# Attention on one Trainium2 core: a turn's score units, projections and small steps in another order

## What is computed

```python
q = (x @ Wq.T + bq).reshape(B, S, H, 2 * hd).transpose(0, 2, 1, 3)   # B 32, S 256, H 16, hd 8
k = (x @ Wk.T + bk).reshape(B, S, H, 2 * hd).transpose(0, 2, 1, 3)
v = (x @ Wv.T + bv).reshape(B, S, H, hd).transpose(0, 2, 1, 3)
q1, q2, k1, k2 = ...                          # two streams, each turned by _apply_rope
s1 = where(causal, neg, q1 k1^T * scale); s2 = where(causal, neg, q2 k2^T * scale)
attn = softmax(s1) - lam * softmax(s2)
out = attn @ v
out = out * rsqrt(mean(out * out) + EPS) * head_norm_w * (1 - LAMBDA_INIT)
x = x + out @ Wo.T + bo                       # x here is layer-normalised before q, k, v
```

## Time and profile before

| | |
|---|---|
| median of 3 runs | 1861.6 us (1861.06 to 1861.72) |
| device time of the profiled execution | 1863.29 us |
| its span, first to last instruction | 1861.6 us |
| mean granted TensorE clock | 0.968 of full speed |
| attention, from the first XT to the last store | about 450 to 1424 us of the span |
| one full turn of attention | 28.53 us |
| busy in the span | PE 86%, DVE 73%, ACT 68%, POOL 56% |

### The profile page before, as it was taken

The page is one execution under the profiler, slowest core; times in us unless marked ns, Lnnn a source line. Parts: engine busy times, 40 slices in busy tenths (PEclk is TensorE's granted clock), DMA queues, the critical chain, the costliest instruction groups (busy, mean ns, idle before and its releaser), DMA issues. The chain is left out here.

```text
span 1861.6 us, 43161 instructions
## 1 busy us (share of the span) xinstructions
PE 1608.8 (86%) x16448; PEld 1220.1 (66%) x16448; DVE 1363.2 (73%) x3442; ACT 1269.4 (68%) x1613; POOL 1046.3 (56%) x707
## 2 busy tenths in 40 slices
PE   4999999994588888888888888888873799999998
PEld 3787777883466666666666666666652577778787
DVE  5777777765778778878887788788742677777775
ACT  4777777772167767767677677677664577777776
POOL 4888888875324434334344343343312688888885
PEclk9999999997699999999999999999996799999999
DMA  3333323321323233232232332322302232233331
GB/s 113 103 114 115 102 88 108 109 103 46 87 79 92 58 91 82 66 94 72 76 94 61 86 87 60 95 78 70 89 12 77 97 115 90 93 114 110 108 109 63
DMA packets 142846, 163.14 MB, mean 88 GB/s; under 512 B 13244, under 2 KB 124558, under 8 KB 141454
## 3 DMA queue, kind: packets, MB, share of 16 engines
q1 hardware_dynamic: 142640, 160.38, 28.8%
HBM read 91.20 MB, written 14.70 MB: 57 GB/s over the span
## 5 line engine op out<-in xcount | busy, mean ns | idle before, releaser
L292 POOL TENSOR_TENSOR ffn_h_low<-ffn_h,ffn_h_high 128x1024 fp32r<-128x1024 f32 x192 | 458.4, 2401 | 95.0 <-ACT ffn_h_high L341 94.8
L1019 ACT ACTIVATE att_prob<-att_ring 128x1024 f32<-128x1024 f32 x384 | 388.6, 1022 | 155.9 <-PE att_ring L1240 153.4
L1125 DVE TENSOR_REDUCE att_nmax<-att_ring 128x4 f32<-128x1024 f32 (+1 forms) x384 | 450.8, 1217 | 54.3 <-PE att_ring L1240 54.3
L479 DVE TENSOR_TENSOR ffn_h<-ffn_up,ffn_comb_wide 128x1024 f32<-128x1024 f32 x256 | 311.3, 1216 | 125.1 <-ACT ffn_up L334 122.8
L334 ACT ACTIVATE ffn_up<-ffn_up 128x1024 f32<-128x1024 f32 x256 | 258.1, 1008 | 202.8 <-PE ffn_up L567 201.1
L341 ACT ACTIVATE ffn_h_high<-ffn_h 128x1024 fp32r<-128x1024 f32 x256 | 269.3, 1052 | 0.7 <-DVE ffn_h L479 0.7
L935 POOL TENSOR_TENSOR att_qk<-att_turned 128x512 f32<-128x512 f32 x64 | 81.4, 1273 | 318.0 <-DVE att_turned L1104 318.0
L1240 PE MATMUL att_ring<-att_qs,att_kd 64*128 64x256 bf16 (+1 forms) x2048 | 151.1, 249 | 95.4 <-DVE att_nmax L1125 57.2
L567 PE MATMUL ffn_up<-ffn_xt_high,ffn_w_high 128*128 128x512 f32 x512 | 214.7, 419 | 1.7 <-DVE ffn_h L479 1.6
L580 PE MATMUL ffn_y<-ffn_h_high,ffn_w_high 128*128 128x512 f32 x512 | 205.3, 401 | 7.0 <-POOL ffn_h_low L292 6.0
L284 POOL TENSOR_TENSOR ffn_ez<-ffn_e_const,ffn_nz 128x16 f32<-128x16 f32 x64 | 185.6, 2901 | 38.2 <-DVE ffn_nz L405 38.2
(11 more groups left out here) (146 smaller groups left out, 2840.7 us busy)
## 6 DMA issues: line engine op xcount, KB each, us to landing
ffn_comb_wide<-ffn_comb_d SPq DMA_DIRECT2D x128, 512.0 KB, 5.6
att_qs<-att_parts SPq DMA_DIRECT2D x192, 128.0 KB, 2.5
att_kd<-att_parts SPq DMA_DIRECT2D x192, 128.0 KB, 2.5
ffn_x<-x SPq DMA_DIRECT2D x32, 256.0 KB, 3.1
ffn_w<-w SPq DMA_DIRECT2D x4, 1024.0 KB, 7.2
x<-ffn_out SPq DMA_DIRECT2D x16, 256.0 KB, 2.4
att_x<-x SPq DMA_DIRECT2D x32, 128.0 KB, 2.3
att_xr<-x SPq DMA_DIRECT2D x32, 128.0 KB, 2.3
```

Of the source, the lines that this page charges most:

```text
L292: nc.gpsimd.tensor_tensor(hts[1][:, e % NH], h[:, e % NH], hts[0][:, e % NH], ALU.subtract).then_inc(low_by_pool, 1)
L479: nc.vector.tensor_tensor(h[:, e % NH], up[:, e % NUP], comb_wide[:, b.c % NW, e].unsqueeze(1).to_broadcast([P, HE, FT]), ALU.mult).then_i ...
L1019: nc.scalar.activation(prob[:, u % NP], ring[:, ORDER.index((kind, u)) % 3], ACT.Exp, scale=SCALE).then_inc(prob_ready, 1)
L1125: nc.vector.tensor_reduce(nmax[:, b, :, h0:h0 + cnt], ring[:, pos % 3] .rearrange("p (s h k) -> p s h k", s=2, k=width), AX.X, ALU.max, ne ...
```

## The change

Two tables are rewritten: `ORDER` (the same 33 units) and `AFTER` (the same steps). Nothing else changes. Cut to the lines with what is spoken of below:

```diff
-ORDER = [("XT", 0), ("T", 6), ("QK", 0), ("NM", 0), ("QK", 1), ("S", 0), ("S", 1), ("T", 7), ("T", 8), ("S", 2),
...
+ORDER = [("XT", 0), ("T", 6), ("QK", 0), ("NM", 0), ("S", 0), ("S", 1), ("T", 7), ("QK", 1), ("S", 2), ("T", 8),
...
-    "rotate 0": ("T", 6), "rotate 1": ("T", 7),
-    "left 0": ("T", 8), "left 1": ("T", 9), "low 0": ("T", 10), "low 1": ("T", 0),
...
+    "rotate 0": ("XT", 0), "rotate 1": ("S", 0), "left 0": ("T", 6), "left 1": ("QK", 1), "low 0": ("T", 11),
+    "low 1": ("S", 9), "high 0": ("S", 1), "high 1": ("S", 3), "mid 0": ("T", 8), "mid 1": ("T", 2),
...
```

More of the change, by code:

```diff
@@ L628 @@
 VW = 32
-ORDER = [("XT", 0), ("T", 6), ("QK", 0), ("NM", 0), ("QK", 1), ("S", 0), ("S", 1), ("T", 7), ("T", 8), ("S", 2),
-         ("S", 3), ("T", 9), ("S", 4), ("T", 10), ("S", 5), ("T", 11), ("S", 6), ("S", 7), ("T", 0), ("V", 0),
-         ("T", 1), ("T", 2), ("NT", 0), ("NT", 1), ("OT", 0), ("S", 8), ("OP", 0), ("S", 9), ("T", 3), ("S", 10),
-         ("T", 4), ("S", 11), ("T", 5)]
+ORDER = [("XT", 0), ("T", 6), ("QK", 0), ("NM", 0), ("S", 0), ("S", 1), ("T", 7), ("QK", 1), ("S", 2), ("T", 8),
+         ("S", 3), ("T", 9), ("S", 4), ("S", 5), ("T", 10), ("T", 11), ("S", 6), ("S", 7), ("T", 0), ("V", 0),
+         ("T", 1), ("T", 2), ("NT", 0), ("NT", 1), ("OT", 0), ("S", 8), ("S", 9), ("T", 3), ("S", 10), ("S", 11),
+         ("T", 4), ("T", 5), ("OP", 0)]
 AFTER = {
[7 rows of a table removed]
[6 rows of a table added]
 }
```

## The result

The changed kernel takes 1907.5 us in the median of 4 runs (1906.75 to 1908.76), the kernel before beside it 1861.7 (1861.06 to 1862.28): a ratio of 1.0245, with an interval of 1.0229 to 1.0262. It is slower by 2.5% where 1.5% was forecast, and 5.5 us beyond the end of the range. Its profiled execution took 1908.76 us, with a span of 1907.0 us, 45.4 more than before's span.

The account below looks back on a forecast made before the run. No engine is full; a chain changing engines bounds each turn. Per turn -0.64 + 0.67 + 0.77 + 0.25 = +1.05 us, over 28 turns +29.4, with the ends +28.6 on 1861.6: 1890 us, range 1870 to 1902.

Parts of the forecast that it names:

- The blocks: Short DVE instructions with two SBUF inputs or SBUF copies stand until POOL's instruction ends: 0.67, 0.77 and 0.25 us per turn.
- 0.67 for newton: Newton's first instruction on DVE stands until POOL ends left 0, so QK 1's read starts later: 0.67 us per turn.
- 0.77 and 0.74 for low 1: NT 1's DVE instruction with both inputs in SBUF falls inside POOL's low 1: forecast 0.77 us per turn.
- 0.25 and 0.20 for normalise: Normalise's first DVE instruction meets POOL's second instruction of streams: between 0 and 0.45 us, taken as 0.25 per turn.
- The rival that nothing blocks: DVE and POOL share access word by word; a turn loses 0.64 us, total 1842 us; chance 0.10.
- the one of newton alone: Only newton is blocked, NT 1 escapes low 1: a turn between 0 and +0.3 us, 1860 to 1869; chance 0.11.
- The waits removed: Waits taken away: DVE for QK 1 0.2, NT 0 for V's read 0.3, the tail 0.15; 0.64 us per turn.
- The tail of the turn: From DVE's start on NT 0 to the next QK 0: 8.75 us instead of 8.91, so 0.15 us less.
- one case of it in which every turn loses 2 us: PE's clock falls after the thin stretch between T 8 and T 11, some 2 us per turn, 1940 us; chance 0.07.
- The ends: First and last turns outside the 28 full ones: turn 2 +0.4, turn 0 +1.5, turns 31 to 33 -2.7 us.
- The -3.3 us of turn 31: In turn 31 T 7 waits for NM instead of S 1; S 0, S 1 and weigh 1 finish before it: -3.3 us.
- For turn 0: S 0, ahead of QK 1, waits for the first DMAs into `kd` and holds QK 1: 0 to 4, taken +1.5 us.

Follow-up runs that it names:

- the pause of 2.24 us: Kernel before's first half with the changed kernel's second half, NM behind QK 1, newton behind S 2 instead of S 1: 1928.5 us, ratio 1.0353.

## Why the prediction was wrong in size

**The blocks: right.** All three are where they were forecast. Newton's and NT 1's instructions end 0.04 and 0.05 us behind POOL's, normalise's first 0.08 (0.53 us long instead of 0.34). The forecast was 0.67 for newton and 0.63 was measured, 0.77 and 0.74 for low 1, and 0.25 and 0.20 for normalise, which was not moved alone (0.20 is what is left of 29.33 - 27.76 = 1.57). QK 1's read stands 5.54 us behind QK 0's, 5.5 forecast. The rival that nothing blocks is out, and so is the one of newton alone. By the Trainium skill (SBUF — State Buffer, section Who interferes with whom) a DVE instruction with two SBUF inputs, or in a two-port mode, contends with GpSimd, and whichever issued first keeps the shared ports for its whole instruction. These rows agree with it; one pair in the feed-forward blocks does not, and stands in the last section.

**The waits removed: right, one term small.** PE no longer waits behind the read of V, nor DVE ahead of QK 1, and S 0 does not wait for its DMAs in a full turn. They are worth 0.77 us instead of 0.64. The tail of the turn was walked at 0.15 and is 0.33. A turn at full clock is therefore +0.80 and not +1.05 longer, which took 7 us off the forecast.

**The clock: the step that failed.** The sum had nothing for the clock. I had the right place, the thin stretch of PE behind T 8, and the pause nearly right (1.6 us forecast, 1.40 measured), but made one case of it in which every turn loses 2 us, and gave that 0.07, because 1.6 is less than half of the 3.75 us of the earlier trace rows. (28 turns of 2 us on 1890 would also be 1946, not 1940.) The case between, in which two of four turns lose 1.0 to 1.2 us, was in no rival. It cost 14.9 us in the 27 intervals and some 1.5 in turn 30. With the pause filled and nearly all else as it was, the kernel took 1897.8 us, inside the range. The pause is itself made by newton's block: S 3 waits for the read of QK 1, which stands behind newton on DVE, and without the block the pause is 0.65 us. The two terms were priced as if they were independent, and they are not: the full turns had no half clock with newton's block undone, and none with the pause filled. The Trainium skill (TensorE: Matmul & The Clock Gate, section HAM oscillation — how this bites in real kernels) tells of a kernel whose bursts with waits between them ran at half clock each time; here it was half of the turns with the changed kernel and all of them only with the pause of 2.24 us.

**The ends: a wrong sign.** Forecast +0.4 + 1.5 - 2.7 = -0.8. Measured are +3.9 at the start; at the end +2.3 belongs to turn 30, a full turn with half clock in it (0.8 of it is the longer turn), and +2.5 to the last three. The -3.3 us of turn 31 came (25.03 us between two reads of NM, 28.19 before). But for turns 32 and 33 I had taken +0.6 without walking the slots of units that are absent there, and they cost 3.1 and 2.6, of the latter 1.9 at half clock. For turn 0 the mechanism was right: 1.5 us taken from a range of 0 to 4, and 2.6 measured; that turns 1 and 2 also fill more slowly was not in the sum beyond 0.4.

So the sum, with sizes as measured: 27 x 0.79 = 21.3, turn 3 0.5, the half clock 14.9, the start 3.9, the end 4.8: 45.4 instead of 28.6. Direction and mechanism of the slower turn held; the size did not, because a second mechanism came on top that hangs on the first, and the ends had the wrong sign. The 7 us by which the turn at full clock was priced too high hid a part of both.

## What to carry to other kernels

When a change makes a short VectorE instruction wait for GpSimd, ask not only what that costs on the chain but which engine is left without work for its length, and whether its clock holds: here newton's block cost 0.63 us a turn, 17 in all, and brought some 15 us of half clock on top. Put short SBUF-only DVE instructions where GpSimd is idle, and read it from their durations by line, not from idle time, since a block counts as busy. And where units share a few slots by position, walk the slots again for the first and the last turns, in which some units are missing: moving one unit gives every unit behind it another slot.
